# Nine one-row matmuls of zeros ahead of each group's picks, in the edge attention of a four-part graph network

## The reference

```python
hn = _batch_norm(h, bn1_g, bn1_b)
Q, K, V = ((hn @ W).reshape(n, 8, 16) for W in (Wq, Wk, Wv))
score = jnp.clip(jnp.einsum('ehd,ehd->eh', K[src], Q[dst]) / np.sqrt(16), -5.0, 5.0)
a = jnp.exp(score - smax[dst])
a = a / asum[dst]                       # asum: segment sum of a over dst
m = V[src] * a[:, :, None]
wV = jax.ops.segment_sum(m, dst, num_segments=n).reshape(n, 128)
h2 = h_in1 + wV @ Wo + bo
```

## Time and profile before

| | us |
|---|---|
| median of 3 runs | 1572.24 (1561.82 to 1579.97) |
| the profiled execution, its own time | 1566.26 |
| its span, first to last instruction | 1564.4 |
| PE, DVE, POOL busy in the span | 1288.4, 788.9, 410.1 |
| mean granted TensorE clock | 0.783 of full |

### The profile page before, as it was taken

How to read it: one execution, slowest core, us unless ns; L and a number is a source line. 1 busy time by engine, 2 the same in 40 slices (tenths; PEclk the granted TensorE clock), 3 DMA queues, 4 the chain that set the end, 5 groups by cost and what they waited for, 6 DMA issues and landing times. The chain is left out here.

```text
span 1564.4 us, 19913 instructions
## 1 busy us (share of the span) xinstructions
PE 1288.4 (82%) x7067; PEld 853.4 (55%) x7067; DVE 788.9 (50%) x2060; ACT 263.0 (17%) x636; POOL 410.1 (26%) x442
## 2 busy tenths in 40 slices
PE   2599999999999979554679679689778798896795
PEld 1477645555555535543457457467566565674453
DVE  4877647545445645533345445445446435444433
ACT  0566612111111111310000000000001000003111
POOL 2000000000000000055564565555556556500000
PEclk9977799999999989766665766655668556657998
DMA  5000060000000000263343343443444334407000
GB/s 146 12 1 1 1 209 0 8 0 8 1 1 20 21 17 1 62 189 101 102 121 86 109 112 101 111 112 102 112 108 118 102 99 112 111 5 181 24 20 22
DMA packets 80233, 108.29 MB, mean 69 GB/s; under 512 B 16368, under 2 KB 65923, under 8 KB 79894
## 3 DMA queue, kind: packets, MB, share of 16 engines
q1 hardware_dynamic: 57045, 50.31, 12.4%
q0 software_dynamic: 20608, 55.20, 12.3%
q10 hardware_dynamic: 2492, 1.61, 0.4%
HBM read 90.98 MB, written 16.09 MB: 68 GB/s over the span
## 5 line engine op out<-in xcount | busy, mean ns | idle before, releaser
L1425 POOL DMA_INDIRECT counts_all<-kv_d,counts_all x416 | 396.4, 953 | 322.0 <-DVE counts_all L1516 176.0
L1604 PE MATMUL bank<-oh,counts_all 128*8 128x88 f32 (+19 forms) x1944 | 390.1, 326 | 97.9 <-issue 96.0
L850 PE MATMUL bank<-counts_all,parts 125*128 (+2 forms) x2100 | 410.5, 354 | 27.2 <-DVE parts L1041 9.7
L1604 PEld LDWEIGHTS bank<-oh,counts_all 128*8 128x8 f32 (+1 forms) x1944 | 259.3, 181 | 214.0 <-issue 190.6
L850 PEld LDWEIGHTS bank<-counts_all,parts 125*128 125x128 f16 x2100 | 191.3, 97 | 230.9 <-issue 16.6
L1578 PE MATMUL bank<-q_win,counts_all 128*128 128x128 f32 x832 | 188.0, 384 | 53.8 <-issue 40.5
L1504 DVE TENSOR_TENSOR counts_all<-counts_all,bank 128x512 f32<-128x512 f32 x104 | 70.9, 681 | 319.3 <-issue 305.3
L1578 PEld LDWEIGHTS bank<-q_win,counts_all 128*128 128x128 f32 x832 | 158.1, 277 | 86.7 <-issue 76.3
L1294 POOL IOTA iota_n<- 128x125 f16 x1 | 0.2, 240 | 587.3 <-POOLq L834 587.3
L1676 ACT ACTIVATE bank<-score 128x32 f32<-128x32 f32 x104 | 20.8, 200 | 586.4 <-DVE score L1511 420.8
L664 PE MATMUL bank<-parts 128*125 128x125 f16 x625 | 100.6, 319 | 10.4 <-DVE parts L596 10.4
(11 more groups left out here) (221 smaller groups left out, 963.8 us busy)
## 6 DMA issues: line engine op xcount, KB each, us to landing
counts_all<-rel_rows_d SPq DMA_DIRECT2D x104, 128.0 KB
counts_d<-counts_all SPq DMA_DIRECT2D x1, 6835.9 KB
q_win<-q_d SPq DMA_DIRECT2D x104, 64.0 KB
counts_all<-kv_d,counts_all POOLq DMA_INDIRECT x416
counts_all<-counts_d SPq DMA_DIRECT2D x1, 6152.3 KB
kv_d<-counts_all SPq DMA_DIRECT2D x6, 448.0 KB
x<-in_x SPq DMA_DIRECT2D x6, 250.0 KB
out<-z SPq DMA_DIRECT2D x6, 250.0 KB
```

Source lines behind the costliest of these rows:

```text
L850: last = T.matmul(agg_ps[p][:, 0:w], pin[:, s, part, :], counts[:, s, bass.ds(b * BLK, w)], start=(s + part == 0), stop=(s + part == NT))
L1425: G.indirect_dma_start(out=out_rows, out_offset=None, in_=table_d, in_offset=bass.IndirectOffsetOnAxis(ap=index, axis=0)).then_inc(signal, 16)
L1604: last = T.matmul(banks_of[b % 2][0:m, lo - b * BLK:hi - b * BLK], lhs, oh32[n % SETS][:, k, lo - s:hi - s], start=False, stop=False, skip ...
```

## The change

At the head of each `pick(n)`, behind its two waits and ahead of its four products, PE runs nine more matmuls. Each multiplies one row of zeros as 128 weights by the same row as 512 columns, in 16-bit floats, into the whole bank that the picks then overwrite, so the outputs do not change. There are 9 x 104 = 936 of them. Nothing else is touched.

```diff
                         pe.wait_ge(ohT_ready, n + 1)
                         if n >= 2:
                             pe.wait_ge(prod_ready, n - 1)
+                        for _ in range(9):
+                            T.matmul(pick_ps[n % 2][:, :], zrow[0:1, 0:C], zrow[0:1, :], start=True, stop=True)
                         for k in range(GRP):
                             last = T.matmul(pick_ps[n % 2][:, k * C:(k + 1) * C], ohT[n % SETS][:, k, :], q_win[n % WINS][:, :],
                                             start=True, stop=True)
```

## The result

The changed kernel takes 1877.7 us (median of 3 runs, 1865.1 to 1877.8) beside 1572.2 us before: 1.193 times as long, 95% interval 1.1825 to 1.2035. 1635 us was forecast, and the range ended at 1720.

The account below looks back on a forecast made before the run. Cycles of POOL's gather bursts and PE's crawls were taken to bound the attention stage; added records cost 0.65 us per group, 101 groups 66 us, so 1566.3 + 66 = 1632, stated as 1635 us; range 1470 to 1720.

Parts of the forecast that it names:

- What bounds the kernel: Attention stage: cycles of POOL gather bursts, PE held back, then catching up; 6.74 us per group modelled, 6.66 measured.
- the pattern of the crawls: Attention stage: PE slows to some 24 records in 11.2 us behind long gather bursts; 18 crawls, 171 us in all.
- a full ring of six: Attention stage: POOL gathers until six group slots are full, then stops, which lets PE recover; pause about 6.1 us.
- PE's added time: Nine products in each pick: 1.92 us at full clock, 3.84 at half; PE's group 5.35 or 9.76 us.
- The 3.4 us from L1586: Upper end for the nine products' time, from lone zero products on that line: 9 x 380 ns.
- The clock: Attention stage: more streamed columns make PE's clock rise sooner after each crawl, from 0.63 to perhaps 0.75.
- Rival B: Attention stage: zeros do not count, clock stays half, 10.4 us per group, 378 us more, about 1945 us; chance 0.08.
- PE's added records: Attention stage: 73.6 records per group, not 55.6, bring the crawl after 1.9 groups, not 2.5; 66 us more.
- rival C: Attention stage: crawl counts groups or signals, not records, so 2.5 groups stay; 12 us more, about 1582 us; chance 0.14.
- the pause and the groups of a cycle: Attention stage: each cycle costs POOL a 6.1 us pause, shared by 3.5 groups before and 2.4 to 2.6 after.
- Rival A: Attention stage: clock stays full, crawls vanish, 5.7 us per group, 97 us less, about 1475 us; chance 0.23.
- The rule on gaps: Skill's advice to avoid idle gaps between PE's matmul bursts; by it the change would pay, which the prediction half accepted.

Follow-up runs that it names:

- e16: Kernel before, no added products, gathers at most three groups ahead instead of six; slower level: 1564.1 us beside 1565.8, ratio 0.9995.
- e1: Changed kernel with its nine products on 128 rows of real data instead of one row of zeros; faster level: 1431.3 us, ratio 1.0354 to the kernel before.
- e15: Changed kernel with its nine one-row products cut from 512 to 8 columns; slower level: 1600.6 us beside 1567.1 before, ratio 1.0247.
- e14: Changed kernel with its nine products on 128 rows of zeros instead of one; slower level: 1573.8 us beside 1567.1 before, ratio 1.0057.
- e2: Changed kernel with its nine products on 128 rows of zeros instead of one; faster level: 1431.3 us, ratio 1.0354 to the kernel before.
- e5: Changed kernel with its nine products on 64 rows of zeros instead of one; slower level (before 1572.8 us): two runs, 1717.4 and 1763.3 us, no ratio.
- e3: Changed kernel with its nine products on one row of real data instead of zeros; faster level: 1852.3 us, ratio 1.3399 to the kernel before.
- e9: Kernel before, no added products, gathers at most three groups ahead instead of six; faster level: 1401.3 us, ratio 1.0114.
- e4: Changed kernel with its nine one-row products cut from 512 to 8 columns; faster level: 1378.9 us, ratio 0.999 to the kernel before.

## Why the prediction was wrong

**What bounds the kernel.** The place was right (the stage alone is 304 us longer), PE's 3.43 and 5.92 us per group were right, and so was the pattern of the crawls on the traces of that level. But the crawls are a property of the level that the run met: on the other POOL binds, and the traces there show at most short crawls, of some 2 to 6 us. Its account of how a burst ends, by a full ring of six, failed with e16. One trace could not tell.

**PE's added time.** Right. 1.92 us at full clock was forecast, and the groups of e1 take 5.27 us against 5.35; 3.84 us at half clock, and 3.94 are measured, so a group takes 9.87 us against 9.76. The 3.4 us from L1586, named as the upper end, were no measure.

**The clock: the step that failed.** I wrote that nine products of 512 columns more than double the columns and that I expected the clock to rise sooner. It fell. Columns were the wrong measure: with the same columns on 128 rows it is 0.99 (0.89 where PE crawls), on 64 rows 0.69, on one row 0.54 or 0.55. So the step put PE's group at a mix of the two clocks, and the runs showed 9.87 us, half clock nearly throughout, which is 304 us more in the stage where the sum had 66. I had noted that no row shows whether one row counts, and then gave the case in which it does not 0.08. My argument against it, that the clock rises wherever records are dense whatever the operands, had no one-row stretch behind it: the long dense stretches of the trace were products on 125 or 128 rows. And the prediction's own spoke against it, since around 1341 us PE was busy without a gap, on 128 rows, and stayed at half clock. With no evidence either way, the unknown deserved near even odds, and the range should have reached to its price of 1945 us.

**Rival B** was the mechanism, and its sum 1945 us against 1878. The difference is the time at full clock that real work still earns after the zeros (0.55, not 0.50) and block work that I had put too high: 974 us for some 100 groups are 9.7 us, not 10.4.

**PE's added records.** This step was right on its count: the added records bring the crawl after 1.8 to 2.0 groups in e15 and 2.0 to 2.1 in e14, for 1.9 forecast, so rival C's 2.5 is out. But the price was mis-sized even where the clock rises: 66 us forecast, 7 measured in e14. The terms at fault are the pause and the groups of a cycle. I took 6.1 us from two bursts picked by eye, and 3.5 groups; the earlier trace rows had the mean pause, 176.0 us in 38 waits, 4.6 us, and so 104/38 = 2.7 groups to a pause. 5.0 + 4.6/2.7 is 6.7 us, so the model met the measured 6.66 by two errors that cancelled, which was luck. And I held the pause fixed. In e15, at a clock of 0.62, it is 214.9/46 = 4.7 us and did stay; in e14, at 0.89, it is 188.7/49 = 3.9 us. At a fixed 4.6 us e14's eleven more pauses would have cost 51 us; its pauses are 13 us more in all. With the change itself the step had no object: at half clock POOL pauses after each group and nothing crawls.

**Rival A** did not come, since the clock did not. The nearest to its 1475 us is e1, 1431 us, but on a quiet level.

**The rule on gaps.** The Trainium skill, "TensorE: Matmul & The Clock Gate", section "Why this matters for your kernels", says to avoid idle gaps between matmul bursts because the clock drops. The runs show that this is not enough: with the change PE had no gap, busy 974.00 of 974.00 us, and its clock was 0.55, lower than the 0.63 that it had with all its crawls. The engine queue of 64 instructions that the same page of the Trainium skill gives was not measured by any run.

## What to carry to other kernels

A product that is to keep TensorE's clock up should drive all 128 rows: of 1, 64 and 128 rows only 128 brought it near full. Zeros will do, and nine such products take 1.94 us where nine of one row took 2.05. Price it as PE's time at full clock, and ask first what a full clock is worth: here nine cost 0.6% to 3.8%, and three changed the time by no more than 2%, since POOL or the crawls set it more than the clock does. Where the odds of a step rest on an untested property of the chip, the range has to reach to both answers, and before a pattern of one trace is taken as the kernel's own, look at a second trace.

## What the runs showed of the hardware

- The granted clock follows the rows that the products drive and not their data: stage clock 0.99 with nine products of 128 rows, of data (e1) or of zeros (e2), 0.69 with 64 (e5), 0.54 with one row of data (e3) and 0.55 with one of zeros. Where PE crawls it is 0.89 with 128 rows (e14). Rows are not all of it: without added products, on 128 rows and 94% busy, it is 0.74 (e9).
- The same program stands at 1383 us or at 1570 us for whole series of runs. At the slower level PE crawls (24 records in 11 us) after some 130 to 150 records run during an unbroken burst of gathers, whether these take 7 or 13 us, and recovers when the gathers stop. At the faster one POOL gathers for some 520 us on end with hardly a crawl (e4). What makes the level is open: the one chip number found at both speaks against the chip alone, the program is the same, and no run here varied anything else. Why PE is held is open too; neither fewer groups ahead (e16) nor a better clock (e14) took it away.
